# Two bias rows of the induced phase: one-row products into PSUM in place of GpSimd additions

## The chip, the core and the metric

The kernel runs on one core of a Trainium2 chip. Each engine has its own instruction stream: TensorE (PE, with weight loads shown apart as PEld), VectorE (DVE), ScalarE (ACT), GpSimd (POOL) and SyncE (SP, which only issues DMAs here). They wait for each other with semaphores, and each works strictly in its own order. TensorE writes its products to PSUM, eight banks of 128 partitions by 512 f32 numbers; VectorE and ScalarE empty the banks, and GpSimd works on SBUF alone. The metric is the time of one execution on the device in microseconds (us).

## The reference

A small model on 8 sequences (items) of 512 tokens: a two-layer banded-attention tower (D = 192), then an induced-set attention block with 128 inducing points (D = 128, 8 heads), then a mixture of 32 experts. The change lies in the second half of the attention block, `_mab(x, h, h, p2)`, for each item:

```python
def _mab(q, k, v, p):
    x = q + _mha(_ln(q, g1, b1), _ln(k, g1, b1), _ln(v, g1, b1), in_w, in_b, out_w, out_b)
    h = _ln(x, g2, b2)
    ff = gelu(h @ l1w.T + l1b) @ l2w.T + l2b
    return x + ff
```

`_mha` ends with `o @ out_w.T + out_b`. The two bias rows of the change are `out_b` and `l2_b` of this block, each of 128 numbers, added to all 512 tokens of an item. The block's result is added to the logits h of the tower, normalised, and goes to the gate of the experts.

## The kernel before

The kernel has three stages: embed and tower, the induced phase (function `induce`), and the experts. The induced phase works through the 8 items m in a software pipeline written out by hand. Time is cut into steps g; an item is PERIOD = 16 steps behind the one before it, and step g does for each item m the piece numbered p = g - 16 m. Every engine walks through the same steps, with the pieces of the older items first. A constant names the step of each piece (Y2 = 83, DOWN2 = 103, ...); an engine's order is the order of these numbers, and nothing else. So in the round in which item m is at Y2, item m-1 is at UP2 (99) and item m-3 scatters its rows (118 to 133).

An item's [512, 128] arrays are held as [128 partitions, NT = 4 tiles, E = 128], so one pass over an item is an instruction of 128x512. TensorE fills three PSUM banks in turn (`dense`, the tiles seam_dbank): `claim` waits until the bank's last content was copied, `filled` and `take` hand it over, `copied` and `wait_copied` give it back.

The pieces around the change, for item m:

- X2 (step 70): VectorE writes x2, the normalised input of the block (L1710), and signals x2_ready.
- X2_BIAS (79): GpSimd adds `out_b` to x2 in place (L1502) and signals x2b_ready.
- O2_T and Y2 (82, 83): TensorE turns the attention output, ScalarE copies it (o2T), TensorE multiplies it with wout (L1120, four products of 128 columns). VectorE adds x2 and writes y2 (L1907), its statistics (L1699, L1702) follow, GpSimd computes the inverse roots (L1446, L1448), and VectorE normalises to yn (L1710).
- Y2_SUM (85): GpSimd waits until item m-1's down2 bank was copied, computes y2b = y2 + h (L1509) and then adds `l2_b` (L1511).
- UP2 (99, 100): TensorE's up products (L1125), two and two, ScalarE's Gelu (L1639).
- DOWN2 (103): TensorE's sixteen down products (L1300); VectorE adds y2b and writes h2 (L1920), with statistics; GpSimd computes two inverse roots (L1454, L1455, L1458); VectorE normalises to zn and x5 (L1710).
- GATE to SLOT (114 to 117): gate products (L1316, L1317), top-2 selection on VectorE (L1756 to L1760, L1943, L1950, and L1946, for whose result ScalarE waits in L1651), slots (L1805, L1808).
- SCATTER (118 to 133): sixteen indirect DMAs issued by GpSimd (L1491).

In the same round as Y2_SUM of item m, item m+3 is at DOWN1 (38): its short root (L1446, L1448, one column) is GpSimd's next work behind y2b, and VectorE's short norm (R1_NORM, written to seam_v) and TensorE's transpose of it (L1114) wait for it.

The rows `erows` hold the bias rows spread over 128 partitions; `onerow` is one partition of 128 ones.

Of the kernel before, what the change touches and what calls it, by code (L numbers as in the profile page):

```python
# [11 lines left out]
ALU, ACT, AX = mybir.AluOpType, mybir.ActivationFunctionType, mybir.AxisListType  # L12

P = 128
B, S = 8, 512
NT = S // P
# [6 lines left out]
E = 128  # L23
IH = E // DH
IF = 512 // P
# [952 lines left out]
def induce(nc, a, outer, shared, seam, xs):  # L978
# [5 lines left out]
    with ExitStack() as ctx:  # L984
        ph = Phase(nc, "induce", ctx, outer)
# [4 lines left out]
        O1_OUT, O1_ROWS, O1_T, Y1, Y1_NORM, Y1_T = 22, 24, 26, 28, 31, 34  # L990
        UP1, DOWN1, R1_NORM, UK, K2, K2_STORE, Q_STACK, K2_STACK = 36, 38, 39, 42, 43, 50, 49, 55
        S2, M2, T2, V2 = (57, 59, 61, 63), 64, (69, 71, 73, 75), (72, 76)
        O2_OUT, O2_ROWS, O2_T, X2, X2_BIAS, Y2 = (73, 77), (75, 79), 82, 70, 79, 83
        Y2_MOM, Y2_NORM, Y2_SUM, Y2_T = 84, 93, 85, 95
        UP2, DOWN2, Z_NORM, X5_NORM, Z_ROWS, Z_T = (99, 100), 103, 106, 106, 108, 110
        GATE, GATE_1, GATE_2, Z_COPY, GATE_EXP, RANK, COEF, SLOT, STORE = 114, 115, 115, 119, 116, 117, 117, 117, 124
# [5 lines left out]
        NH, NV2 = 7, 3  # L1002
# [6 lines left out]
        erows = seam.wvo0[:, :].rearrange("p (b w e) -> p b w e", b=2, w=3)  # L1009
# [14 lines left out]
        onesr = shared.onerow[:, :].bitcast(F32)  # L1024

        def some(n, name, shape, dt=F32):
# [15 lines left out]
        h = list(seam.h)  # L1042

        scores, turned, dense, obank = seam.scores, seam.turned, seam.dense, seam.obank
# [3 lines left out]
        fore_set, consts_set, scaled = (ph.sem(n) for n in ("fore_set", "consts_set", "scaled"))  # L1048
        ones_in = [ph.sem(f"ones_in{j}") for j in range(2)]
        moments, roots, normed = ph.sem("moments"), ph.sem("roots"), ph.sem("normed")  # L1050
        x2_ready, x2b_ready, y1b_ready, x5_ready = (
            ph.sem(n) for n in ("x2_ready", "x2b_ready", "y1b_ready", "x5_ready"))
        split_hi, q1_hi, k2_hi = ph.sem("split_hi"), ph.sem("q1_hi"), ph.sem("k2_hi")
        q1_out, q1_in, kq_out, k2_out = (ph.sem(n) for n in ("q1_out", "q1_in", "kq_out", "k2_out"))
        k1_in, q2_in, k2_in = ([ph.sem(f"{n}{j}") for j in range(2)] for n in ("k1_in", "q2_in", "k2_in"))
# [10 lines left out]
        BV, BOUT, BL2 = range(3)  # L1066
# [42 lines left out]
        def on_tensor(pe, obank_left=None):  # L1109
# [7 lines left out]
            def by_rows(key, lhs, rhs, n=NT):  # L1117
                bank = dense.claim(pe, key)
                for t in range(n):
                    mm = pe.matmul(bank[:, t * E:t * E + E], lhs[:, t * P:t * P + P], rhs, start=True, stop=True)  # L1120
                dense.filled(mm, key)

            def by_features(key, w, rhs):
                bank = dense.claim(pe, key)
# [72 lines left out]
            def pieces(m, p):  # L1197
                if p == M1:
                    for head in (IH - 2, IH - 1):
                        scores.wait_copied(pe, ("s1", m, head))  # L1200
                    bank = dense.claim(pe, ("m1", m))
                    dense.filled(pe.transpose(bank[0:IH, 0:P], peak1[:, :], ident[:, :]), ("m1", m))
                if p == M2:
                    for head in (IH - 2, IH - 1):
                        scores.wait_copied(pe, ("s2", m, head))
                    bank = dense.claim(pe, ("m2", m))
                    dense.filled(pe.transpose(bank[0:IH * NT, 0:P], peak2[:, :], ident[:, :]), ("m2", m))
                if p == A_X:
                    pe.wait_ge(normed, norm_order[FINAL, m])
                    for k in range(KT):  # L1210
                        bank = dense.claim(pe, ("fT", m, k))
                        for t in range(NT):
                            mm = pe.transpose(bank[0:DP, t * P:t * P + P], xs[m][:, t, k * DP:k * DP + DP], ident[:, :])
                        dense.filled(mm, ("fT", m, k))
                if p == A_H:
                    for k in range(KT):
                        dense.wait_copied(pe, ("fT", m, k))
                    bank = dense.claim(pe, ("logits", m))
                    for t in range(NT):
                        for k in range(KT):  # L1220
                            mm = pe.matmul(bank[:, t * E:t * E + E], xT[:, k, t * P:t * P + P], wc[:, k, :],
                                           start=(k == 0), stop=(k == KT - 1))
# [12 lines left out]
                if p == O1_ROWS:  # L1235
                    outs.wait_copied(pe, ("o1", m))
                    bank = dense.claim(pe, ("o1R", m))
# [13 lines left out]
                if p == UP1:  # L1251
                    pe.wait_ge(ffn_in, FFN)
                    dense.wait_copied(pe, ("t1T", m))
                    bank = dense.claim(pe, ("up1", m))
# [27 lines left out]
                    turn(("o2T", m), o2)  # L1282
                if p == Y2:
                    dense.wait_copied(pe, ("o2T", m))
                    by_rows(("y2", m), o2T, wout[:, 1, :])
                if p == Y2_T:
                    pe.wait_ge(normed, norm_order[ATT2, m])
                    turn(("t2T", m), yn)
# [4 lines left out]
                if p == DOWN2:  # L1293
                    for c in range(IF):
                        dense.wait_copied(pe, ("up2", m, c))
                    bank = dense.claim(pe, ("down2", m))
                    for t in range(NT):
                        out = bank[:, t * E:t * E + E]
                        for c in range(IF):
                            mm = pe.matmul(out, hid2[:, c, t * P:t * P + P], l2[:, 1, c, :],  # L1300
                                           start=(c == 0), stop=(c == IF - 1))
                    dense.filled(mm, ("down2", m))
                if p == Z_T:
                    pe.wait_ge(normed, norm_order[FF2, m])
# [128 lines left out]
        def on_gpsimd(pool, chain=0, v_left=None):  # L1433
# [26 lines left out]
            def step(g):  # L1460
# [33 lines left out]
                for m, p in items(g):  # L1494
                    if p == Y1 + 1:
                        dense.wait_copied(pool, ("y1", m))
                        if m:
                            dense.wait_copied(pool, ("down1", m - 1))
                        pool.tensor_tensor(y1b[:, :], y1[:, 0, :], erows[:, 0, BL2, :], ALU.add).then_inc(y1b_ready, 1)
                    if p == X2_BIAS:  # L1500
                        pool.wait_ge(x2_ready, m + 1)
                        pool.tensor_tensor(x2[:, :, :], x2[:, :, :],  # L1502
                                           erows[:, 1, BOUT:BOUT + 1, :].broadcast_to([P, NT, E]), ALU.add)\
                            .then_inc(x2b_ready, 1)
                    if p == Y2_SUM:
                        dense.wait_copied(pool, ("y2", m))
                        if m:
                            dense.wait_copied(pool, ("down2", m - 1))
                        ch.mark(pool.tensor_tensor(y2b[:, :, :], y2[:, :, :], h[m % NH][:, :, :], ALU.add))  # L1509
                        ch.after()  # L1510
                        pool.tensor_tensor(y2b[:, :, :], y2b[:, :, :],  # L1511
                                           erows[:, 1, BL2:BL2 + 1, :].broadcast_to([P, NT, E]), ALU.add)\
                            .then_inc(y2b_ready, 1)
                    if p == Z_ROWS:
                        zm = z[m % 2]
                        if m == 0:
                            pool.wait_ge(late_in, LATE)
                        if m >= 2:
                            pool.wait_ge(scattered[m % 2], 16 * NT * SLOTS * (m // 2))
                        pool.wait_ge(normed, norm_order[FF2, m])  # L1520
                        first = zm[:, :, 0, 0:E]
                        ch.mark(pool.tensor_tensor(first, zn[:, :, :], grows[:, 0:1, :].broadcast_to([P, NT, E]),
                                                   ALU.mult))
                        ch.after()
                        pool.tensor_tensor(first, first, grows[:, 1:2, :].broadcast_to([P, NT, E]), ALU.add)\
                            .then_inc(z_ready, 1)
                        pool.tensor_scalar(zm[:, :, :, E:E + 1].bitcast(I32), ids[:, :, :, None], m * S * SLOTS, None,
                                           ALU.add).then_inc(z_named, 1)
                    if p == GATE:
                        pool.wait_ge(x5_ready, m + 1)  # L1530
                        if m:
                            pool.wait_ge(base_out, 16 * m)
                        pool.tensor_tensor(base[:, :, :], h2[:, :, :], x5[:, :, :], ALU.add).then_inc(base_ready, 1)
# [153 lines left out]
        def on_vector(dve, chain=0, x_final=None, xT_left=None, kq_left=None):  # L1687
# [125 lines left out]
            def pieces(m, p):  # L1813
# [88 lines left out]
                if p == Y2:  # L1902
                    bank = dense.take(dve, ("y2", m))
                    if m:
                        dve.wait_ge(y2b_ready, m)
                    dve.wait_ge(x2b_ready, m + 1)
                    dense.copied(dve.tensor_tensor(wide(y2), bank[:, :], wide(x2), ALU.add), ("y2", m))  # L1907
                if p == Y2_MOM:
                    dense.wait_copied(dve, ("y2", m))
# [598 lines left out]
```

## Time and profile before

| | |
|---|---|
| median of 3 runs | 2302.05 us (2300.82 to 2307.59) |
| profiled execution, its own time | 2290.77 us |
| its span, from the first to the last instruction | 2289.0 us |
| PE, PEld busy | 1994.3 us (87%), 1440.8 us (63%) |
| DVE, ACT, POOL busy | 1331.5 us (58%), 1171.7 us (51%), 779.3 us (34%) |
| mean granted TensorE clock | 0.909 |

Busy times are averages over the whole span. The three stages have different limits, so they are read by stretches. The granted clock is the share of full speed: 1.00 is 2.4 GHz and 0.50 is 1.2 GHz, and a mean between them is a mixture in time. In a timeline the columns are start, duration, engine, line, operation and tiles, with the count of merged instructions, and in brackets the engine's idle time before and what ended it. An f32 product leaves two records, so four products of one weight tile are eight records. "issue" is time in which the engine waited for nothing that the profile shows.

### The profile page before, as it was taken

The numbers are of one execution on the slowest core, as the hardware profiler recorded it, in microseconds if no ns is written. First come the engines' busy times: TensorE is split into PE (matmuls) and PEld (weight loads), VectorE is DVE, ScalarE is ACT, GpSimd is POOL, SyncE is SP. The second block draws the span as 40 slices with busy tenths as digits, with TensorE's granted clock in tenths as the row PEclk, the third lists the DMA queues.
The fourth block names the chain that finished last, engine by engine and source line by source line (L and its number), as shares of the span: only waits on it lengthen the run. The fifth ranks groups of instructions, "written<-read, shape, count | busy, mean of one in ns | idle before, by whom it ended". The sixth has DMA issues, their size and how long they took to land. (4 is left out here: it accounts for less than half of the span.)

```text
span 2289.0 us, 44262 instructions
## 1 busy us (share of the span) xinstructions
PE 1994.3 (87%) x14601; PEld 1440.8 (63%) x14601; DVE 1331.5 (58%) x4494; ACT 1171.7 (51%) x2507; POOL 779.3 (34%) x973
## 2 busy tenths in 40 slices
PE   5699999999999999999998878888876459999986
PEld 4366666666666666666666546656554349999973
DVE  2365565556556655565566645777766625555547
ACT  2376666566666665665666324555644224444434
POOL 0012221222122212221223221234787745555556
PEclk8799999999999999999999885798877579999995
DMA  3642441244134513440350124342321277777654
GB/s 101 123 72 28 70 71 38 34 70 70 33 40 70 94 30 43 70 69 27 47 88 11 34 70 83 86 92 49 80 57 37 76 247 234 231 228 228 200 157 129
DMA packets 113846, 207.06 MB, mean 90 GB/s; under 512 B 23060, under 2 KB 47510, under 8 KB 112968
## 3 DMA queue, kind: packets, MB, share of 16 engines
q1 hardware_dynamic: 100632, 182.97, 36.0%
q0 software_dynamic: 10176, 17.09, 2.3%
q10 hardware_dynamic: 2816, 4.16, 0.6%
q8 instruction: 124, 2.03, 0.4%
q14 instruction: 98, 0.80, 0.1%
HBM read 147.53 MB, written 64.66 MB: 93 GB/s over the span
## 5 line engine op out<-in xcount | busy, mean ns | idle before, releaser
L733 ACT ACTIVATE tower_prob<-tower_prob,tower_negmax 128x386 f32<-128x386 f32 (+1 forms) x768 | 390.5, 556 | 312.0 <-DVE tower_negmax L943 311.4
L943 DVE CUSTOM_DVE_ANT_0 tower_prob<-seam_sbank,tower_band 128x386 f32<-128x386 f32 (+1 forms) x768 | 346.1, 488 | 138.7 <-PE seam_sbank L496 133.3
L534 PEld LDWEIGHTS seam_tbank<-sh_ident,tower_prob 128*128 128x128 f32 x1920 | 226.3, 142 | 131.0 <-issue 81.0
L534 PE MATMUL seam_tbank<-sh_ident,tower_prob 128*128 128x128 f32 x1920 | 283.0, 278 | 23.5 <-DVE seam_probT L968 21.3
L789 ACT ACTIVATE seam_probT<-seam_tbank 128x384 f32<-128x384 f32 (+1 forms) x576 | 227.5, 430 | 123.6 <-PE seam_tbank L534 121.3
L2186 POOL DMA_INDIRECT scratch_yt<-experts_y,experts_rows x190 | 186.7, 983 | 183.6 <-DVE experts_y L2329 151.1
L473 PE MATMUL seam_dbank<-tower_oxT,tower_w 96*128 96x512 f32 x384 | 190.9, 621 | 14.7 <-ACT tower_oxT L778 14.7
L496 PE MATMUL seam_sbank<-seam_k_st,seam_q_st 49*128 49x386 f32 (+1 forms) x768 | 160.1, 411 | 30.0 <-POOL seam_k_st L684 16.3
L2244 PE MATMUL experts_ybank<-experts_w,experts_hid 128*128 128x128 f32 x1520 | 185.1, 275 | 0.0
L2232 PE MATMUL experts_hbank<-experts_zT,experts_w 128*128 128x256 f32 x760 | 181.5, 382 | 1.1 <-ACT experts_zT L2268 1.1
L2277 ACT ACTIVATE experts_hid<-experts_hbank,experts_w 128x256 f32<-128x256 f32 x190 | 79.8, 471 | 193.9 <-PE experts_hbank L2232 193.9
L2244 PEld LDWEIGHTS experts_ybank<-experts_w,experts_hid 128*128 128x128 f32 x1520 | 177.2, 192 | 0.1
L700 POOL TENSOR_TENSOR tower_glob<-tower_vglob,tower_prob 128x102 f32<-128x102 f32 x128 | 46.8, 365 | 338.6 <-ACT tower_prob L733 224.2
L2232 PEld LDWEIGHTS experts_hbank<-experts_zT,experts_w 128*128 128x128 f32 x760 | 138.3, 192 | 16.7 <-issue 1.7
L393 PE MATMUL seam_dbank<-tower_w,tower_hid 128*128 128x192 f32 x768 | 141.0, 334 | 4.5 <-DVE tower_hid L917 4.5
L513 PE MATMUL seam_obank<-seam_probT,seam_v 128*17 128x128 f32 x3840 | 142.8, 276 | 1.6 <-DVE seam_probT L968 1.6
L2314 DVE TENSOR_SCALAR experts_hid<-experts_hbank,experts_w 128x256 f32<-128x256 f32 x190 | 83.2, 479 | 103.6 <-PE experts_hbank L2232 103.6
L1491 POOL DMA_INDIRECT scratch_zs<-induce_z,induce_slot x128 | 127.5, 996 | 36.6 <-issue 34.3
L496 PEld LDWEIGHTS seam_sbank<-seam_k_st,seam_q_st 49*128 49x128 f32 x768 | 73.9, 184 | 98.5 <-issue 85.3
L412 PE MATMUL seam_dbank<-seam_xT,seam_wqk 96*96 96x512 f32 x256 | 129.4, 632 | 5.6 <-ACT seam_xT L748 5.6
L393 PEld LDWEIGHTS seam_dbank<-tower_w,tower_hid 128*128 128x128 f32 x768 | 123.1, 190 | 17.8 <-issue 9.6
L1547 ACT ACTIVATE seam_probT<-seam_tbank 128x512 f32<-128x512 f32 x128 | 69.6, 597 | 100.6 <-PE seam_tbank L1182 64.2
(329 smaller groups left out, 3441.0 us busy)
## 6 DMA issues: line engine op xcount, KB each, us to landing
experts_w<-ew SPq DMA_DIRECT2D x95, 578.0 KB, 4.0
scratch_qk<-seam_qk SPq DMA_DIRECT2D x64, 384.0 KB, 4.7
seam_q_st<-scratch_qk SPq DMA_DIRECT2D x96, 192.0 KB, 8.3
seam_k_st<-scratch_qk SPq DMA_DIRECT2D x96, 192.0 KB, 11.6
experts_rows<-scratch_zs SPq DMA_DIRECT2D x95, 132.0 KB
scratch_kq<-seam_qk SPq DMA_DIRECT2D x8, 1024.0 KB, 4.3
experts_res<-scratch_yt SPq DMA_DIRECT2D x8, 1024.0 KB, 7.9
seam_q_st<-scratch_kq SPq DMA_DIRECT2D x48, 128.0 KB, 4.3
```

Source lines behind the costliest of these rows:

```text
L393: mm = pe.matmul(bank[:, j * D:(j + 1) * D], lhs[:, k, t * P:t * P + P], rhs[:, k, :], start=(k == 0), stop=(k == kts - 1))
L412: mm = pe.matmul(bank[0:DP, :], wqk[layer][:, w, k, c * DP:c * DP + DP], xT[:, k, :], start=(k == 0), stop=(k == KT - 1))
L473: mm = pe.matmul(bank[:, :], w1[:, k, c * P:c * P + P], oxT[:, k, :], start=(k == 0), stop=(k == KT - 1))
L496: mm = pe.matmul(bank[:, 0:width(i)], stack(q_st[j], h0 + e)[:, i * P:i * P + P], stack(k_st[j], h0 + e)[:, first_key(i):first_key(i) + wi ...
L513: mm = pe.matmul(obank[32 * e:32 * e + W17, c:c + P], v[nq % 2][:, t, h0 + e, :], probT[(2 * gq + e) % PT][:, jb * P:jb * P + P], start=(j ...
L534: mm = pe.transpose(bank[:, jb * P:jb * P + P], prob[:, hg % PR, at + jb * P:at + jb * P + P], ident[:, :])
L733: act.activation(prob[:, hg % PR, 0:width(i)], prob[:, hg % PR, 0:width(i)], ACT.Exp, bias=negmax[:, hg % PR:hg % PR + 1], scale=-1.0).the ...
L789: turned.copied(act.activation(probT[(2 * (g - 1) + e) % PT][:, 0:at], bank[:, 0:at], ACT.Copy), ("t", g - 1, e))
L943: scores.copied(dve.tensor_tensor_reduce(prob[:, hg % PR, 0:width(i)], bank[:, 0:width(i)], band[:, BAND_AT[i]:BAND_AT[i] + width(i)], sca ...
L2186: pool.indirect_dma_start(out=a["yt"], out_offset=bass.IndirectOffsetOnAxis(ap=rows[q % ZB][:, h, E:E + 1].bitcast(U32), axis=0), in_=y[q ...
L2232: mm = pe.matmul(bank[:, j * TB:j * TB + TB], w[q % WW][:, W1 + c * P:W1 + c * P + P], zT[q % 2][:, :], start=True, stop=True)
L2244: mm = pe.matmul(bank[:, h * E:h * E + E], hid[q1 % 2][:, c, h * P:h * P + P], w[q1 % WW][:, W2 + c * E:W2 + c * E + E], start=(c == 0), s ...
```

## The change

GpSimd's two additions of a bias row (L1502 and L1511, once an item) go. In their place TensorE starts the bank of y2, and that of down2, with one product: a column of ones (one partition, 128 weights) times the bias row (one partition, 128 numbers, read four times over, 512 columns), which writes the whole bank. The products that follow accumulate on it. VectorE's y2 addition waits for x2_ready in place of x2b_ready. No step number is moved.

```diff
@@ step numbers
-        O2_OUT, O2_ROWS, O2_T, X2, X2_BIAS, Y2 = (73, 77), (75, 79), 82, 70, 79, 83
+        O2_OUT, O2_ROWS, O2_T, X2, Y2 = (73, 77), (75, 79), 82, 70, 83
@@ TensorE
+            def on_rows(bank, row):
+
+                pe.matmul(bank[:, :].rearrange("p (t e) -> p t e", e=E), onesr,
+                          erows[0:1, 1, row:row + 1, :].broadcast_to([1, NT, E]), start=True, stop=False,
+                          skip_group_check=True)
...
                 if p == Y2:
                     dense.wait_copied(pe, ("o2T", m))
-                    by_rows(("y2", m), o2T, wout[:, 1, :])
+                    bank = dense.claim(pe, ("y2", m))
+                    on_rows(bank, BOUT)
+                    for t in range(NT):
+                        mm = pe.matmul(bank[:, t * E:t * E + E], o2T[:, t * P:t * P + P], wout[:, 1, :],
+                                       start=False, stop=True, skip_group_check=True)
+                    dense.filled(mm, ("y2", m))
...
                     bank = dense.claim(pe, ("down2", m))
+                    on_rows(bank, BL2)
                     for t in range(NT):
                         out = bank[:, t * E:t * E + E]
                         for c in range(IF):
                             mm = pe.matmul(out, hid2[:, c, t * P:t * P + P], l2[:, 1, c, :],
-                                           start=(c == 0), stop=(c == IF - 1))
+                                           start=False, stop=(c == IF - 1), skip_group_check=True)
@@ GpSimd
-                    if p == X2_BIAS:
-                        pool.wait_ge(x2_ready, m + 1)
-                        pool.tensor_tensor(x2[:, :, :], x2[:, :, :],
-                                           erows[:, 1, BOUT:BOUT + 1, :].broadcast_to([P, NT, E]), ALU.add)\
-                            .then_inc(x2b_ready, 1)
                     if p == Y2_SUM:
                         dense.wait_copied(pool, ("y2", m))
                         if m:
                             dense.wait_copied(pool, ("down2", m - 1))
-                        ch.mark(pool.tensor_tensor(y2b[:, :, :], y2[:, :, :], h[m % NH][:, :, :], ALU.add))
-                        ch.after()
-                        pool.tensor_tensor(y2b[:, :, :], y2b[:, :, :],
-                                           erows[:, 1, BL2:BL2 + 1, :].broadcast_to([P, NT, E]), ALU.add)\
+                        pool.tensor_tensor(y2b[:, :, :], y2[:, :, :], h[m % NH][:, :, :], ALU.add)\
                             .then_inc(y2b_ready, 1)
@@ VectorE
                     if m:
                         dve.wait_ge(y2b_ready, m)
-                    dve.wait_ge(x2b_ready, m + 1)
+                    dve.wait_ge(x2_ready, m + 1)
                     dense.copied(dve.tensor_tensor(wide(y2), bank[:, :], wide(x2), ALU.add), ("y2", m))
```

## Rows read from the trace of the kernel before

**Rows 1.** Windows: busy us (and count) of each engine, granted clock, DMA share, GB/s.

```profile
core 0: us, PE busy (x) PEld busy (x) DVE busy (x) ACT busy (x) POOL busy (x), PEclk, DMA share, GB/s
1450.00:1735.00 285.00, 235.78 (x1712) 164.48 (x1715) 212.96 (x663) 158.28 (x271) 148.71 (x172) 0.82 0.31 69
1735.00:1850.00 115.00, 46.18 (x215) 34.70 (x207) 61.09 (x207) 27.29 (x35) 89.26 (x92) 0.63 0.27 84
1850.00:2289.00 439.00, 403.08 (x2566) 353.55 (x2566) 227.98 (x683) 174.52 (x452) 226.72 (x231) 0.91 0.67 207
```

**Rows 2.** Timeline of POOL at the end of the induced phase.

```profile
1845.91 0.95 POOL L1491 DMA_INDIRECT scratch_zs<-induce_z,induce_slot  x1 [0.30 <-issue]
1850.06 0.10 POOL L2180 MEMSET experts_half<- 128x8 f32 x1 [3.19 <-POOLq L984]
```

**Rows 3.** Waits of DVE from 1370 to 1850 us: us in total, times, longest.

```profile
DVE induce_zn L1710 <- POOL seam_padrow_f L1458: 22.2, 7, 5.3
...
DVE seam_v L1710 <- POOL seam_padrow_f L1448: 14.2, 8, 2.4
DVE induce_h L1920 <- PE seam_dbank L1300: 11.0, 6, 3.7
```

**Rows 4.** Timeline of all engines, item 2's h2 and item 3's y2b.

```profile
1620.40 0.69 DVE L1920 TENSOR_TENSOR induce_h<-seam_dbank,induce_y2b 128x512 f32<-128x512 f32 x1 [1.49 <-PE seam_dbank L1300]
...
1621.24 1.26 POOL L1509 TENSOR_TENSOR induce_y2b<-induce_y,seam_qk_f 128x512 f32<-128x512 f32 x1 [4.13 <-DVE induce_h L1920]
...
1622.59 1.26 POOL L1511 TENSOR_TENSOR induce_y2b<-induce_y2b,seam_wvo 128x512 f32<-128x512 f32 x1
...
1623.82 0.23 POOL L1446 TENSOR_SCALAR seam_padrow_f<-seam_padrow_f 128x1 f32<-128x1 f32 x1
...
1624.85 0.35 DVE L1710 TENSOR_SCALAR seam_v<-seam_v,seam_padrow_f 128x128 f32<-128x128 f32 x1 [2.43 <-POOL seam_padrow_f L1448]
...
1625.25 0.48 PE L1114 MATMUL seam_dbank<-sh_ident,seam_v 128*128 128x128 f32 x1 [2.66 <-DVE seam_v L1710]
```

**Rows 5.** Timelines of DVE, POOL and ACT where L1502 or L1511 runs.

```profile
1492.51 3.15 DVE L1710 TENSOR_SCALAR induce_x<-seam_qk_f,seam_padrow_f 128x128 f32<-128x128 f32 x4
...
1509.25 2.13 DVE L1710 TENSOR_SCALAR induce_yn<-induce_y,seam_padrow_f 128x128 f32<-128x128 f32 x4
...
1678.00 0.32 DVE L1758 TENSOR_TENSOR induce_ga<-induce_ga,induce_rank 128x160 f32<-128x160 f32 x1
...
1680.15 1.86 DVE L1758 TENSOR_TENSOR induce_gb<-induce_gb,induce_rank 128x160 f32<-128x160 f32 x1
...
1680.54 1.28 POOL L1502 TENSOR_TENSOR induce_x<-induce_x,seam_wvo 128x512 f32<-128x512 f32 x1
...
1722.58 0.22 ACT L1651 ACTIVATE induce_gs<-induce_gs 128x20 f32<-128x20 f32 x1 [1.48 <-DVE induce_gs L1946]
```

**Rows 6.** Timeline of PE: two f32 products of 512 columns, at either clock.

```profile
1520.05 1.99 PE L1125 MATMUL seam_dbank<-induce_t,induce_l 128*128 128x512 f32 x4
1521.87 1.05 PE L1120 MATMUL seam_dbank<-induce_wout,induce_o2T 128*128 128x128 f32 x8
...
1604.05 3.63 PE L1125 MATMUL seam_dbank<-induce_t,induce_l 128*128 128x512 f32 x4
```

**Rows 7.** Line L424 in the tower: duration ns min/median/max, first and last start.

```profile
L424 PE MATMUL seam_dbank<-seam_padrow,sh_onerow x16: 489/494/501, 50.5 to 1163.1; 1*128 1x512 f32 x16
```

**Rows 8.** Timelines around y2: DVE in item 2, PE and ACT in item 4.

```profile
1569.79 0.69 DVE L1907 TENSOR_TENSOR induce_y<-seam_dbank,induce_x 128x512 f32<-128x512 f32 x1 [2.11 <-PE seam_dbank L1120]
...
1646.01 1.88 PE L1125 MATMUL seam_dbank<-induce_t,induce_l 128*128 128x512 f32 x4
...
1648.86 1.27 ACT L1639 ACTIVATE induce_hid<-seam_dbank,induce_l1b 128x512 f32<-128x512 f32 x2
```

**Rows 9.** Windows behind two gaps of TensorE, columns as in Rows 1.

```profile
1499.00:1502.00 3.00, 2.41 (x20) 1.81 (x20) 2.24 (x7) 0.94 (x3) 0.00 (x0) 1.00 0.60 233
...
1587.00:1593.00 6.00, 5.00 (x27) 3.00 (x26) 4.28 (x12) 1.86 (x5) 5.01 (x7) 0.50 0.25 83
```

**Rows 10.** Timeline of PE behind item 0's y2b.

```profile
1498.67 0.27 PE L1202 MATMUL seam_dbank<-sh_ident,seam_rows 128*8 128x128 f32 x1 [1.57 <-DVE seam_qk L1716]
```

More of the change, by code:

```diff
@@ L1050, in induce @@
         moments, roots, normed = ph.sem("moments"), ph.sem("roots"), ph.sem("normed")
-        x2_ready, x2b_ready, y1b_ready, x5_ready = (
-            ph.sem(n) for n in ("x2_ready", "x2b_ready", "y1b_ready", "x5_ready"))
+        x2_ready, y1b_ready, x5_ready = (ph.sem(n) for n in ("x2_ready", "y1b_ready", "x5_ready"))
         split_hi, q1_hi, k2_hi = ph.sem("split_hi"), ph.sem("q1_hi"), ph.sem("k2_hi")
```

## The prediction

> **What bounds the kernel now.** I read the busy shares by stage first [rows 1]. The first 1370 us (embedding and tower) and the last 439 us (the experts) hold none of the changed instructions, so the change is worth what it does between 1450 and 1850 us. There no engine is full. From 1450 to 1735 us TensorE is busy 235.8 of 285 us at a granted clock of 0.82 (its two levels are 1.2 and 2.4 GHz, so about a third of that stretch is at the lower one), VectorE 213.0 and GpSimd only 148.7. From 1735 to 1850 us GpSimd leads with 89.3 of 115 us. The stage ends with GpSimd's last scatter, and the experts' first GpSimd instruction comes 3.2 us behind it [rows 2]. So the path goes from engine to engine, and the waits have to be read.
>
> The waits of VectorE in this stage [rows 3] show GpSimd as a link: 22.2 us in 7 waits before zn and 14.2 us in 8 before the short norms, both for the inverse roots that GpSimd computes; and 11.0 us in 6 waits on the second down product. One item in order of time [rows 4] shows how they hang together. VectorE waits 1.49 us for L1300 and makes h2 (L1920). Only then may GpSimd start the next item's y2b (L1509; it had waited 4.13 us). It adds the bias (L1511), and only then comes to the root (L1446) that VectorE has been waiting for: 2.43 us. TensorE, behind VectorE, has stood idle for 2.66 us. The removed L1511 stands in this chain with nothing beside it. L1502, the other removed addition, lies elsewhere, before the y2 addition.
>
> **What the change removes.** L1511, 8 times. In [rows 4] the root starts at 1623.82; without L1511 it would start at the end of L1509, 1622.50: 1.3 us. Items 1 to 7 have this order, items 1 to 4 with a short root next and items 5 to 7 with the root of zn. VectorE's wait of 2.43 us is longer than 1.3 us, as are the seven before zn on average (22.2/7 = 3.2 us), so the gain is passed on whole: 7 x 1.3 = 9.1 us. If the released root then waits for something else, the gain is nothing; that is the other bound.
>
> L1502, 8 times about 1.28 us. GpSimd rarely makes anybody wait with it, but VectorE suffers under it [rows 5]: its L1758 of 128x160, otherwise 0.32 us, takes 1.86 us when L1502 starts inside it. Four more items (3, 4, 6, 7) show one such VectorE instruction of 1.8 to 2.1 us there. In most of them the y2 addition behind it has to wait for TensorE in the new kernel anyhow, so I count nothing. Three places count. In item 6 the stall reaches ScalarE, which waits 1.48 us for VectorE; I take 1.2 us. In item 1 four norms take 2.13 us in place of 1.1 and TensorE waits for them 0.85 us: 0.8. In item 0 four norms take 3.15 us beside both y2b additions, half of the 2.0 us too much being L1511's: 1.0. Together 3.0 us; bounds 0 and 5 x 1.5 + 1.0 + 1.0 = 9.5.
>
> **What it adds.** Sixteen products of one row by 128x512, f32. No row of this kernel has one. The nearest are the 128-row products L1125 [rows 6]: two of them are four records (an f32 product leaves two), and the next product starts 1.82 us after the first, so 0.91 us each at 2.4 GHz; at 1.2 GHz the same four take 3.63 us in place of 1.99, some 1.7 us each. A one-row product exists in the tower, L424, in the one-pass type: its one record lasts 494 ns [rows 7], while one of the 128-row L1125 lasts about 0.6, so the missing rows save little. I take 0.91 and bound it by 0.49 below and 1.7 above. The Trainium skill, "TensorE: Matmul & The Clock Gate", section Back-to-back issue gap, gives about 216 ns for 512 columns at the upper clock; taken for each of the two records that would be an estimate of 0.43 us for a product, and the sum below would be some 5 us better. The trace has 0.455 us per record, about double, and it decides.
>
> The product ahead of down2 stands between the up products' copies, which TensorE waits for first, and L1300. Behind it are VectorE's h2, y2b and the roots. Paid eight times: 8 x 0.91 = 7.3 us. In two of the eight h2 does not wait for TensorE (6 waits in [rows 3]), so some of the product is covered there: minus 0.9.
>
> The product ahead of y2 stands behind the wait for o2T. Queued behind it on TensorE are the second pair of up products and the next scores. In items 0, 1 and 2 VectorE waits for TensorE at y2 already (2.11 us in item 2 [rows 8]) and TensorE runs on without a gap, so it is paid: 0.91 + 0.91 + 1.7 (item 2 has the lower clock there) = 3.5 us. In items 3 to 7 there is cover: in item 4 the second up pair ends at 1647.89, but ScalarE, loading activation tables, copies it only from 1648.86, 0.97 us later [rows 8], more than 0.91. Without this cover it would be another 5 x 0.91 = 4.6 us.
>
> The accumulating start=False changes no count of products. The y2 addition now waits for x2_ready, VectorE's own norm 13 steps earlier: nothing. The y2b semaphore comes earlier.
>
> Sum: -9.1 - 3.0 + 7.3 - 0.9 + 3.5 = -2.2 us. The profiled execution has 2290.8 us with a span of 2289.0, so 2288.6; the runs' median stands 11.3 us above it, so the same sum is made against the median: 2302.05 - 2.2 = 2299.8 us. I call anything within 0.3% (6.9 us) no change, about what a measurement of this kernel can tell.
>
> **Rivals.**
>
> *A, the clock stays up: faster.* In the 2.66 us gap of [rows 4] and the three like it (items 1, 2, 4) the granted clock falls to 1.2 GHz and stays there for 6 to 9 us; from 1587 to 1593 us TensorE is busy 5.0 of 6 us at 0.50 [rows 9]. In item 0's round the same gap was 1.57 us [rows 10], and the clock stayed at 1.00 [rows 9]. The change makes 2.66 into about 1.35. If all four falls go, some 4 x 5.0 us of work take half the time; of the 10 us I count 7 to 8, as part ends in other waits: 2299.8 - 7.5 = 2292. Against it: the clock also falls in gapless stretches of transposes and narrow gate products, so a fall may only come later. The same page of the Trainium skill, section The HAM clock gate, says that idleness lowers the clock and sustained activity restores it, by which shorter gaps and more products both help; the fall in a 2.66 us gap agrees, and no row shows whether a one-row product counts as activity.
>
> *B, TensorE pays more: slower.* Place: the product ahead of L1300. It pays for itself only while it costs less than the 1.3 us that L1511 gives back. If TensorE is at 1.2 GHz there, it costs 1.7 us: 8 x 0.8 = 6.4 us more, and if the cover at y2 is gone too, 4.6 more. 2299.8 + 6.4 + 4.6 = 2310.8. It decides from about 1.5 us a paid product on. For it: the clock is low at the start of the last down products. Against it: in items 0 to 3 L1300 runs at 2.4 GHz.
>
> *C, the roots are not freed:* the gap behind L1509 is filled by a wait on VectorE's statistics and the 9.1 us shrink to half: 2304. Against it: the short root's statistics are long done in [rows 4]. It stays within 0.3%.
>
> **How the numbers follow.** My sum, with C and halves of A and B, stays within 0.3%: 0.47. A whole, or a bias product that is cheaper than its 128-row kin: 0.33. B: 0.20. Range: low end below A, 2288; high end at B, 2312. The likeliest case alone: 2295 to 2306.
>
> **What the profile after would show.** L1502 and L1511 gone, 32 new one-row records of 0.5 to 0.6 us. VectorE's waits before zn down from 22.2 to about 13 us and before the short norms from 14.2 to about 9 or 10; TensorE's gaps of 2.66 us and the like near 1.4. VectorE's wait for L1300 up from 11.0 by some 5 us. The 1.8 to 2.1 us VectorE instructions before y2 back at 0.3. The granted clock from 1450 to 1735 us: 0.82 in my sum, 0.88 or more under A, under 0.80 under B. I am wrong if the shortened wait reappears at the next link, if the new products bunch where nothing covers them, or if the clock moves by its own timing.

## The result, and the profile after

The changed kernel takes 2308.8 us (median of 15 executions) against 2298.9 us for the one before (15 executions): 1.0055 times as long, 95% interval 1.0035 to 1.0074 (the medians alone give 1.0043, which lies inside). That is slower by more than the 0.3% that I called no change. The time lies inside the range, 9.0 us above the value I gave, on the side of rival B, which had the smallest chance (0.20).

The profiled execution of the changed kernel took 2321.6 us, 13 us above its median, and the one of before stood 8 us below its own. So the two profiles exaggerate: they differ by 31 us, the medians by 10. They show where the time goes, not how much; a second profile of the changed kernel, which differs from this one, stands under experiment 2.

Windows of the changed kernel, columns as in [rows 1]:

```profile
1450.00:1735.00 285.00, 254.82 (x1623) 168.78 (x1622) 185.53 (x593) 144.41 (x251) 112.60 (x139) 0.75 0.30 64
1735.00:1850.00 115.00, 80.29 (x339) 55.78 (x335) 71.53 (x252) 42.32 (x55) 84.97 (x90) 0.65 0.13 43
```

Against [rows 1], TensorE is busier (254.8 us for 235.8) and has got through fewer instructions (1623 for 1712), although it has the bias products besides. The granted clock goes with both: 0.75 in place of 0.82. VectorE and GpSimd were busy for less of the same time (185.5 us for 213.0, and 112.6 for 148.7), GpSimd in part because its additions are gone.

Waits of VectorE in the changed kernel, 1370 to 1850 us, as in [rows 3]:

```profile
DVE induce_h L1923 <- PE seam_dbank L1311: 28.9, 8, 6.2
...
DVE induce_y L1910 <- PE seam_dbank L1293: 22.1, 7, 6.9
DVE induce_zn L1713 <- POOL seam_padrow_f L1469: 15.9, 6, 3.7
...
DVE seam_v L1713 <- POOL seam_padrow_f L1459: 7.7, 7, 1.1
```

The bottom two rows are the intended effect. The wait before the short norms falls from 14.2 to 7.7 us, the longest from 2.4 to 1.1 us, by the 1.3 us of L1511. The wait before zn falls from 22.2 to 15.9 us. The top two are the price: the wait for the down product goes from 11.0 to 28.9 us, and the y2 addition, for which the waits of before had 5.5 us in three items, now waits 22.1 us in seven.

Two f32 records make a product. Line L1124 of the changed kernel between 1450 and 1850 us: busy us, mean ns of a record:

```profile
L1124 PE MATMUL seam_dbank<-seam_wvo,sh_onerow 1*128 1x512 f32 x32 | 24.2, 845 | 3.1 <-ACT induce_hid L1642 3.1
```

and two such pairs in its timeline, one at each clock:

```profile
1485.52 1.12 PE L1124 MATMUL seam_dbank<-seam_wvo,sh_onerow 1*128 1x512 f32 x2
1486.57 1.16 PE L1293 MATMUL seam_dbank<-induce_wout,induce_o2T 128*128 128x128 f32 x8
1487.66 0.69 PE L1162 MATMUL seam_sbank<-seam_q_st 48*128 48x512 f32 x2
...
1626.08 2.07 PE L1124 MATMUL seam_dbank<-seam_wvo,sh_onerow 1*128 1x512 f32 x2
```

The projection starts 1.05 us after the bias product: that is its price at 2.4 GHz (I had 0.91). All 32 records make 24.2 us of TensorE's time, 1.5 us a product. That leaves the clock to look at. Windows of the changed kernel around that first product and in its longest stretches at 1.2 GHz:

```profile
1480.00:1487.00 7.00, 6.76 (x76) 4.79 (x76) 5.24 (x17) 3.69 (x9) 2.04 (x3) 1.00 0.02 5
1488.00:1491.00 3.00, 3.00 (x26) 2.38 (x28) 3.00 (x10) 0.61 (x3) 0.00 (x0) 0.50 1.08 148
1505.00:1528.00 23.00, 23.00 (x136) 16.37 (x128) 13.08 (x37) 9.16 (x16) 3.55 (x7) 0.50 0.39 56
1601.00:1630.00 29.00, 26.71 (x143) 18.51 (x144) 17.00 (x42) 13.49 (x22) 17.73 (x20) 0.50 0.36 90
1690.00:1716.00 26.00, 26.00 (x95) 16.25 (x93) 18.18 (x58) 11.20 (x16) 19.09 (x20) 0.50 0.35 76
```

In this profile the clock falls behind the first product although TensorE had been busy 6.76 of 7 us, and it stays low for 23 to 29 us at a time with TensorE busy nearly all through. In the profile of before, from 1485 to 1798 us, the low stretches last 3 to 10 us, but for two of 17 and 20. A low clock beside a busy TensorE is not new, though. The kernel before has it ahead of these items, where no bias product runs:

```profile
1437.00:1460.00 23.00, 21.68 (x152) 17.31 (x154) 16.49 (x47) 9.95 (x19) 4.58 (x8) 0.50 0.46 92
```

So two theories stand. **Added work**: TensorE pays the products' own time, and the clock is an accident. **Clock**: the one-row products make the granted clock fall more often than their own time explains, and everything behind them pays.

### The profile page after: what moved, and what is told of

It is laid out like the page before. It is cut to its first block and busy times, and to the rows that moved or that the text cites. A ratio compares the mean times of both kernels' runs of the same rounds, so it can differ in the third digit from the quotient of the medians.

```text
span 2319.8 us, 44310 instructions
## 1 busy us (share of the span) xinstructions
PE 2047.1 (88%) x14633; PEld 1465.1 (63%) x14633; DVE 1323.5 (57%) x4494; ACT 1173.1 (51%) x2507; POOL 758.2 (33%) x957
## 5 line engine op out<-in xcount | busy, mean ns | idle before, releaser
L1502 POOL DMA_INDIRECT scratch_zs<-induce_z,induce_slot x128 | 127.1, 993 | 37.4 <-issue 35.2
```

## The experiments

Each ratio is against the kernel before, timed on the same chip beside the experiment. From group to group the kernel before moved by more than the effect: 2328.5, 2326.3, 2300.4, 2298.1 and 2299.7 us in the five groups below. A price in us is the ratio's distance from 1, or from another ratio, times about 2300 us, unless it is said to be from medians.

**1. The halves, the gain alone, the price alone.** e1 has the product and the freed GpSimd for y2 only, e2 for down2 only. e3 leaves both biases out of the computation. e4 keeps GpSimd's additions and throws the products away:

```diff
 # shortened. e3: no product, no addition; e4, on the kernel before:
-                    on_rows(bank, BOUT)
-                    on_rows(bank, BL2)
+ pe.matmul(bank, onesr, row, start=True, stop=True)   # ahead of both projections
+ ... projections with start=True: they overwrite it
```

> The change's first half alone: the output projection's bias goes into PSUM as a one-row product and GpSimd's addition to x2 is gone; GpSimd keeps the addition of the second bias to y2b. The change as a whole measured 1.0055 times before. Three theories. (1) Added work: each product costs its own time on TensorE at the clock of the moment (a pair of records took 1.12 us at 2.4 GHz and 2.07 us at 1.2 GHz in the profile after), nothing else. Of y2's eight products nearly all are paid, since the later profile shows VectorE waiting for TensorE at y2 in seven of eight items: +9 to +13 us, less 3 us for the removed addition's stalls: ratio 1.003 to 1.004. (2) Clock: a one-row product is a stretch in which TensorE counts as idle, and the granted clock falls more often after it: more than the products' own time is lost, ratio 1.004 or more, and the granted clock of 1450 to 1735 us falls below 0.79. (3) My prediction's terms: +3.5 - 3.0 = +0.5 us, ratio 1.000.

> The second half alone: the bias of the last projection goes into PSUM as a one-row product, GpSimd's second addition on y2b is gone; the addition to x2 stays with GpSimd and y2 has no product. (1) Added work: eight products of 0.9 to 2 us by the clock, +8 to +13 us, against 1.3 us x 7 that the root comes earlier: ratio 0.999 to 1.002. (2) Clock: as for the first half, ratio above 1.003 with a granted clock below 0.79 in 1450 to 1735 us. (3) My prediction's terms: -9.1 + 7.3 - 0.9 = -2.7 us, ratio 0.999.

> Leaves work out: neither bias of the induced phase is added by anyone (no one-row products, no additions on GpSimd). What is left is what freeing GpSimd is worth. By my prediction's terms -9.1 - 3.0 = -12 us, ratio 0.995. If GpSimd's additions lay beside other work, 1.000. With the added-work theory this run and the next one should add up to the change as a whole: (ratio here - 1) + (ratio of the next - 1) = 0.0055. If the sum is far less than the change, the two halves meet: an earlier root brings TensorE's work together where the products then stand in the way.

> The kernel before, with both one-row products put ahead of the projections and overwritten by them (the projections start their banks anew), and GpSimd's additions all kept: the price of the products alone. (1) Added work: 16 products of 0.9 to 2.07 us, most of them paid: +14 to +22 us, ratio 1.006 to 1.010, granted clock of 1450 to 1735 us about as before (0.80 to 0.84). (2) Clock: ratio above 1.010, granted clock below 0.79. (3) My prediction's terms: +7.3 + 3.5 = +10.8 us at most, ratio 1.0047 or less.

Measured: e1 1.0007 (0.9990 to 1.0024), e2 1.0000 (0.9981 to 1.0018), e3 0.9933 (0.9908 to 0.9958), e4 1.0086 (1.0061 to 1.0111). Freeing GpSimd is worth 15.6 us (11.7 by medians) where I had 12.1. The products cost 20 us where I had 9.9. Each half fits my terms (+0.5 and -2.7 us) within its interval; the whole does not, and is not the sum of its halves. Both theories have misses here. Added work fits e2 and e4, but for e1 it asked for 1.003 to 1.004, above the interval. The clock theory's values were missed in e1 (1.004 or more), e2 (above 1.003) and e4 (above 1.010, just inside the interval); the clocks that it asked for from 1450 to 1735 us, below 0.79, came in the profiles of e2 and e4 (0.78 each) and not in that of e1 (0.82).

**2. Rows and places.** Beside the changed kernel again (e5), e6 makes the same products from 128 rows: weights of 1/128 and the bias from every partition, the same 512 columns.

```diff
-                pe.matmul(bank[:, :].rearrange("p (t e) -> p t e", e=E), onesr,
-                          erows[0:1, 1, row:row + 1, :].broadcast_to([1, NT, E]), start=True, stop=False,
+                pe.matmul(bank[:, :].rearrange("p (t e) -> p t e", e=E), share[:, :],
+                          erows[:, 1, row:row + 1, :].broadcast_to([P, NT, E]), start=True, stop=False,
```

e7 issues the one-row products ahead of the waits:

```diff
-                    dense.wait_copied(pe, ("o2T", m))
                     bank = dense.claim(pe, ("y2", m))
                     on_rows(bank, BOUT)
+                    dense.wait_copied(pe, ("o2T", m))
```

(and the same for down2's four waits). e8 has no product at all: on the kernel before, GpSimd adds the second bias to h ahead of time.

```diff
+                        pool.tensor_tensor(h[m % NH], h[m % NH], BL2 row, ALU.add)   # shortened; behind L1502
-                        pool.tensor_tensor(y2b, y2b, BL2 row, ALU.add)               # L1511
```

> The changed kernel itself, on the chip of the three runs after it, so that they stand beside it. The first call gave 1.0007 for y2's half, 1.000 for down2's half, 0.9933 with both biases left out and 1.0086 with the products alone: products and freed GpSimd add up to 1.0019, the halves to 1.0007, and the whole had measured 1.0055 on another chip. If the pieces add up, this run gives 1.001 to 1.003; if the halves hurt each other, 1.0045 to 1.0065 again.

> The change, with the same 16 products made of all 128 rows (weights of 1/128, the bias from every partition) in place of one row: the same columns, the same two records a product, 128 times as many cells at work. (1) Added work: a product costs what it did, but for a weight load of 128 rows: within 0.15% of the changed kernel. (2) Clock: if one-row products count as idleness to whatever grants the clock, the granted clock of 1450 to 1735 us rises from below 0.79 to 0.82 or more and the time falls by 10 us or more, ratio 0.4% below the changed kernel's.

> The change, with each product issued ahead of the waits that it stood behind: y2's before the wait for o2T's copy, down2's before the waits for the four Gelus. The work of every engine is the same, only its place moves. (1) Added work on the path between the last copy and the first product of the projection: taking it off that path gives back nearly all, since TensorE waits there in any case: ratio 0.993 to 0.997. If TensorE had no wait there (it arrives late itself), the product costs the same at either place and the ratio stays that of the changed kernel. (2) Clock by one-row products: ratio above 1.002, as the products are still there.

> No product on TensorE at all: the second bias is added by GpSimd to h, ahead of time, right behind the addition to x2, so that only one addition is left between y2 and y2b. It asks for the part of my sum that frees the root of the last norm alone: -9.1 us there, and one more early GpSimd addition of 1.3 us beside VectorE (+0 to +3 us of stalls): ratio 0.996 to 0.9985. If what the run without biases gained came from the other addition, ratio 1.000.

Measured: e5 1.0041 (1.0016 to 1.0066), e6 0.9941 (0.9918 to 0.9963), e7 0.9991 (0.9969 to 1.0013), e8 0.9954 (0.9932 to 0.9975). The 128-row products make the same change 1.0% faster, where added work alone allowed 0.15%. e8 measures one term of my sum alone: -10.6 us, where I had -9.1 before any stall of the moved addition. e7 says that the place matters too: some 12 us of the one-row products' price go when they are issued in the wait (7 us by medians). That was neither theory's value: added work asked for 0.993 to 0.997, or for no change, and the clock theory for more than 1.002.

The products' busy time is not what changed. Line L1124 of e5, then of e6, between 1450 and 1850 us:

```profile
L1124 PE MATMUL seam_dbank<-seam_wvo,sh_onerow 1*128 1x512 f32 x32 | 21.6, 760 | 3.1 <-ACT induce_hid L1642 3.1
```

```profile
L1124 PE MATMUL seam_dbank<-seam_wvo,induce_share 128*128 128x512 f32 x32 | 21.5, 760 | 3.5 <-ACT induce_hid L1644 2.1 <-issue 1.4
```

But the next product starts a little sooner behind 128 rows, here at 2.4 GHz, e5 and then e6:

```profile
1525.63 1.12 PE L1124 MATMUL seam_dbank<-seam_wvo,sh_onerow 1*128 1x512 f32 x2
1526.68 1.16 PE L1293 MATMUL seam_dbank<-induce_wout,induce_o2T 128*128 128x128 f32 x8
```

```profile
1523.36 1.02 PE L1124 MATMUL seam_dbank<-seam_wvo,induce_share 128*128 128x512 f32 x2
1524.22 1.05 PE L1294 MATMUL seam_dbank<-induce_wout,induce_o2T 128*128 128x128 f32 x8
```

That is 1.05 us behind one row and 0.86 behind 128 (0.96 at other places); at 1.2 GHz it is 2.00 against 1.71 to 1.87. With 16 products at 0.09 to 0.29 us each I estimate 1 to 5 us from this, of the 19 us between e5 and e6.

The clock of these two profiles does not show what the theory asked for. e5 is the changed kernel again, in an execution 7 us below its median; e6's is 7 us below its own too. The stretch of the items in e5, then the 43 us from its first bias product on:

```profile
1485.00:1800.00 315.00, 261.03 (x1648) 175.86 (x1646) 210.03 (x687) 155.39 (x256) 156.55 (x181) 0.79 0.25 57
1492.00:1535.00 43.00, 38.58 (x341) 25.34 (x339) 33.39 (x100) 29.00 (x55) 11.12 (x17) 1.00 0.51 95
```

The stretch of the items in e6:

```profile
1485.00:1800.00 315.00, 262.83 (x1677) 178.53 (x1676) 218.48 (x726) 163.04 (x266) 172.52 (x197) 0.79 0.26 60
```

Both stand at 0.79, and from 1450 to 1735 us at 0.81 and 0.82, where the theory wanted e5 below 0.79. Behind e5's first product, at 1492.39 us, the clock does not fall: it holds 1.00 to 1535 us. So the fall behind the first product in the profile after is one execution's, not the rule. From 1485 us up to the last scatter (1874 and 1853 us) the clock is 0.74 in e5 and 0.76 in e6, which makes 202 and 177 us at 1.2 GHz.

**3. How far the rows carry.** e9 is e4 with 128 rows, e10 the change with 32 rows (`share[0:32, :]`, weights of 1/32), e11 has y2's bias by a 128-row product and the second as in e8, e12 is e6 with the products ahead of the waits as in e7.

> The kernel before with 16 products of 128 rows added and overwritten, GpSimd's additions kept: the run that gave 1.0086 (+20 us) with one-row products, with rows changed alone. (1) Added work: the columns and records are the same, so the price is the same: ratio 1.006 to 1.011. (2) Clock: in the change as a whole 128 rows in place of one gave 0.9941 against 1.0041; if that is the clock, which counts a one-row product as little or no work, the price here falls to less than half, ratio 1.000 to 1.004, with the granted clock of 1485 to 1800 us higher than with one-row products at the same place.

> The change with products of 32 rows. (2) Clock, by share of the rows at work: between one row (1.0041) and 128 rows (0.9941), ratio 1.000 to 1.003. If a threshold in rows decides and 32 are enough, 0.992 to 0.996; if 32 are as bad as one, 1.002 to 1.006. (1) Added work: no dependence on rows at all, and then the 128-row run's 0.9941 must have been something else.

> A candidate for the best version: y2's bias by a 128-row product on TensorE, the second bias added to h by GpSimd ahead of time in the place of the addition to x2, so TensorE has eight products instead of sixteen and the root of the last norm has one addition ahead of it. The 128-row version gave 0.9941, the h version 0.9954, both biases left out 0.9933. Expected 0.992 to 0.996; if 128-row products gain by themselves (they keep the clock up), this is worse than the 16-product version, 0.995 or more.

> The 128-row version with each product issued ahead of the waits of its projection. With one-row products the move took 1.0041 to 0.9991. (1) Added work: the products of the 128-row version are still on the path, so the move gives 5 us or so again: ratio 0.990 to 0.993. (2) Clock: the waits before the projections are filled with work that counts, ratio also 0.990 to 0.993 and a granted clock above 0.80 in 1485 to 1800 us. If the 128-row version already pays nothing for its products (it stood 0.0008 above the version without biases), the move changes nothing: 0.993 to 0.996.

Measured: e9 1.0064 (1.0042 to 1.0087), e10 1.0019 (0.9999 to 1.0040), e11 0.9953 (0.9935 to 0.9971), e12 0.9962 (0.9948 to 0.9977). 32 rows are slower than 128 clear of the intervals; that they are faster than one is not (1.0019 against 1.0055, 1.0041 and 1.0032), and the next product starts 1.05 us behind them, as behind one row. The place, worth 12 us to one-row products, is worth nothing to 128-row ones. But e9 missed: with GpSimd's additions in place, the rows are worth 0.2% as measured (1.0086 against 1.0064 in two groups of runs, the intervals overlap), not the half of the price that the clock theory asked for. (The granted clock from 1485 to 1800 us did go up, 0.75 to 0.78.)

**4. Was it the rows?** e6 also has one more tile, one more memset and one more wait. h13 has all three and takes one row of that tile. h14 repeats the 128-row version, h15 the kernel before. h16 has one row for y2 and 128 for down2.

```diff
-                          ... share[:, :],   erows[:, 1, row:row + 1, :].broadcast_to([P, NT, E]),
+                          ... share[0:1, :], erows[0:1, 1, row:row + 1, :].broadcast_to([1, NT, E]),
```

> Everything that the 128-row version has beside the rows (a tile of 64 KB more in SBUF ahead of the others, its memset, the wait at y2), with products of one row of that tile. If the rows decide: 1.003 to 1.007, as the changed kernel. If the layout or the memset made the 128-row version fast: 0.992 to 0.997.

> The 128-row version again: 0.992 to 0.997 if its 0.9941 stands. A value of 1.000 or more would make its first measurement chance.

> The kernel before against itself: 1.000, within 0.003 either way. Where it lies outside, differences of 0.3 per cent in this series say nothing.

> Both products, y2's with one row, down2's with 128. Behind down2 TensorE has other items' work, ahead of it the longest wait (four Gelus). If the rows of both matter alike: half way, 0.998 to 1.001. If down2's product decides: 0.993 to 0.997. If y2's does: 1.002 to 1.006.

Measured: h13 1.0032 (1.0007 to 1.0057), h14 0.9966 (0.9950 to 0.9981), h15 0.9986 (0.9969 to 1.0003), h16 0.9984 (0.9972 to 0.9997). It was the rows: h13's interval and h14's do not touch. The kernel before against itself shows how much 0.14% is worth. The profile of h13 repeats the waits of the first profile of the changed kernel to 0.1 us; both are of long executions, h13's the longest of its ten. In e5 the same two waits are 23.4 and 13.4 us, in e6 17.9 and 8.5. Waits of VectorE, h13 and then h14:

```profile
DVE induce_h L1925 <- PE seam_dbank L1312: 28.9, 8, 6.2
...
DVE induce_y L1912 <- PE seam_dbank L1294: 22.1, 7, 6.9
```

```profile
DVE induce_h L1925 <- PE seam_dbank L1312: 18.4, 7, 4.3
...
DVE induce_y L1912 <- PE seam_dbank L1294: 14.0, 7, 3.4
```

**5. Which product, and what is left of the price.** h17 is the mirror of h16. h18 is e3 again.

> 128 rows for y2, one row for down2. One row for y2 and 128 for down2 gave 0.9984, half way between 0.9955 (mean of the two 128-row runs) and 1.0043 (mean of the three one-row runs). If the two products weigh alike, 0.998 to 1.002 here too; if down2's one-row product carries most of it, 1.001 to 1.004; if y2's does, 0.994 to 0.997.

> Leaves both biases of the induced phase out, no products and no additions, as before. If the 128-row products cost their own time (16 x 1.1 us, half of it covered), this is 0.3 to 0.5 per cent below their version: 0.990 to 0.993. If they are nearly free, 0.993 to 0.996.

Measured: h17 1.0004 (0.9984 to 1.0023), h18 0.9937 (0.9914 to 0.9961). Waits of VectorE in h18:

```profile
DVE induce_zn L1707 <- POOL seam_padrow_f L1463: 19.1, 7, 4.9
...
DVE induce_h L1917 <- PE seam_dbank L1305: 15.0, 6, 3.4
DVE seam_v L1707 <- POOL seam_padrow_f L1453: 8.8, 8, 1.1
...
DVE induce_y L1904 <- PE seam_dbank L1119: 5.5, 4, 2.5
```

Now the price has a floor to be measured from, 0.9935 (mean of e3 and h18):

| version | ratio | above the floor | mean granted clock, less that of before in the same group |
|---|---|---|---|
| no bias (e3, h18) | 0.9933, 0.9937 | 0 | +0.0031, +0.0018 |
| 128 rows (e6, h14) | 0.9941, 0.9966 | 0.0019 = 4 us | +0.0049, +0.0019 |
| 1 row y2, 128 rows down2 (h16) | 0.9984 | 0.0049 = 11 us | +0.0021 |
| 128 rows y2, 1 row down2 (h17) | 1.0004 | 0.0069 = 16 us | -0.0007 |
| 1 row (after, e5, h13) | 1.0055, 1.0041, 1.0032 | 0.0108 = 25 us | -, -0.0021, -0.0025 |

The clock is the mean over a whole execution, averaged over the 7 to 33 executions of each. Taking the eight products of one bias from 128 rows to one costs 7 to 14 us, for down2 (12 and 14 us) clear of the intervals; for y2 (7 and 9 us) they overlap. The clock goes down with it in three of the four steps; from h14 to h16 it does not (+0.0019 and +0.0021, in the same group).

The window from 1485 to 1800 us holds the eight items. In h18, h15 (before), h14 and h13:

```profile
1485.00:1800.00 315.00, 252.66 (x1723) 180.55 (x1723) 227.62 (x758) 166.61 (x273) 181.72 (x209) 0.81 0.28 64
```

```profile
1485.00:1800.00 315.00, 248.36 (x1674) 175.23 (x1673) 228.99 (x729) 163.97 (x267) 192.06 (x213) 0.80 0.26 60
```

```profile
1485.00:1800.00 315.00, 265.16 (x1695) 180.48 (x1695) 220.91 (x728) 164.56 (x268) 171.25 (x196) 0.79 0.26 60
```

```profile
1485.00:1800.00 315.00, 277.56 (x1567) 184.24 (x1567) 201.75 (x670) 154.49 (x253) 152.19 (x176) 0.72 0.25 57
```

From h14 to h13 the clock goes from 0.79 to 0.72, and TensorE gets through 1567 products where it had 1695. Of these 128, though, some 80 are the work of 1485 to 1491 us in h14, where the items start 6 us later (first bias product at 1492.5 us, for 1486.5 in h13); some 50 are left. And e5, with the same one-row products, stood at 0.79. The means over all executions are the better witness, and they point the same way by less. A mean lower by 0.0044 (0.9049 in h14, 0.9005 in h13), at a low level of half speed, is 0.0044 x 2300 / 0.5 = 20 us more at 1.2 GHz, in which TensorE gets 10 us less done. From e6 to e5 it is 0.0069 (0.9012, 0.8943): 32 us and 16 us. The times differ by 17.5 and 19.3 us (medians). These are estimates of the most that the clock can explain, as if every such microsecond delayed the end. So the clock is large enough for most of the difference; the earlier start behind 128 rows has 1 to 5 us of it by my estimate; and items that arrive late may stand in each other's way. The three were not separated. Nor does a long low stretch need a one-row product; h18 has no bias product at all:

```profile
1665.00:1685.00 20.00, 19.92 (x89) 14.55 (x88) 13.89 (x40) 7.86 (x13) 16.26 (x17) 0.50 0.31 66
```

## Why the prediction was wrong

**What the change removes.** Right, and sized a little low: 12.1 us predicted, 14.5 and 15.6 measured (h18, e3; 14.1 and 11.7 by medians); the part of L1511 alone 9.1 predicted, 10.6 measured (e8). Its signs came too: the wait before the short norms at 7.7 us (I gave 9 to 10), the one before zn at 15.9 us (about 13), TensorE's gaps of 2.7 to 3 us down to 1.20, 1.31 and 1.70 us.

**What it adds.** Here the prediction failed, at the step that follows "the missing rows save little": the price of the 128-row kin, 0.91 us, was made the price of the one-row product, +9.9 us in the sum. The sentence itself holds, the missing rows save nothing; they cost. The next product starts 1.05 us behind one row and 0.86 to 0.96 us behind 128, and the whole kernel is 17 to 19 us slower with one row. With the kin itself in its place, 16 products cost 4 us, less than my 9.9, so more of them was covered than I had counted; with one row they cost 25 us. VectorE's wait for L1300, for which I gave 5 us more, took 17.9 more in the first profile. The bounds, 0.49 and 1.7 us a product, were bounds of the product's own time and did not hold the cost. I had written that no row shows whether a one-row product counts as activity, and then gave the question to rival A's benefit only, for which more products were to help.

**The cover at y2.** I had it in items 3 to 7, under ScalarE's table loads. The y2 addition waits in seven items in the first profile of the changed kernel, and with 128 rows in seven (h14, 14.0 us in all) or four (e6, 8.5 us), against 5.5 us without biases (h18). So this cover was an error too, but a small one in time: with 128 rows the whole price is 4 us.

**Rival A, the clock stays up.** Wrong in its step from gap to fall. The gaps became short as it asked, and even without any product (h18, e3) the clock from 1485 to 1800 us is 0.81 and 0.79 against 0.80 before. The falls stay or move. And the changed kernel has the lower clock; it stands at 0.50 for 23 us with TensorE busy 23.00 of them. The Trainium skill, "TensorE: Matmul & The Clock Gate", section The HAM clock gate, ties the clock to how busy TensorE has been. By busy time alone that stretch would not stand at 0.50, so the trace disagrees, and it decides. I had also written that I am wrong if the clock moves by its own timing. In part it does: the same kernel fell behind its first product in one profile and held 1.00 there in another (e5).

**Rival B, TensorE pays more.** It gave 2310.8 us and a granted clock under 0.80; measured were 2308.8 and 0.75, but 0.81 in e5's profile. Both conditions are seen in part in the first profile: eight of the sixteen products meet the low clock, and y2's cover is gone in seven items. But its mechanism, the products' own time at 1.2 GHz, applies nearly as well to 128 rows (1.71 to 1.87 us against 2.00), which cost 4 us. So its number came close by luck: it named the place, not the cause. Rival C did not happen: the roots are freed.

**What stays open.** Why rows matter little while GpSimd's additions remain (e4 and e9, 0.2% with overlapping intervals), and with that why the halves cost 0 to 2 us and the whole 7 to 13. And the link itself: that the rows act through the clock is argued, from the mean clock measured lower in both pairs. Against it stand the equal 0.79 of e5's and e6's profiles and the step from h14 to h16. A lower clock can also be in part the effect of a kernel that waits more, and no run held the clock fixed. The later start behind 1 and 32 rows is a rival for part of the price that no run removed.

**The better versions.** With 128 rows the change does what it was meant to, as measured against the kernel before: 0.9941 and 0.9966. The one without TensorE (e8, 0.9954) and the mixed one (e11, 0.9953) are as good, and cannot be told apart from it here. All lie within 0.4% of the floor.

## What to carry to other kernels

The price of a product is more than the time that it occupies TensorE: in a kernel whose TensorE moves between 1.2 and 2.4 GHz, look also at the mean granted clock over many executions, since two profiles of one kernel can differ (0.72 and 0.79 here). Try a bias product from all 128 rows (weights of 1/128, the bias on every partition) beside the one-row form: here it had the same busy time and took 0.7 and 1.0% off the kernel's time. When such a change is priced, a run that leaves the work out altogether gives the floor, and one that adds the work alone gives the price; halves that look free say nothing of the whole.

## What the runs showed of the hardware

The granted clock stood at 0.50 for 23 and 26 us in which TensorE was busy all the time (changed kernel, 1505 to 1528 and 1690 to 1716 us), and for 20 us in which it was busy 19.92, with no bias product in the kernel (h18, 1665 to 1685 us). The number of rows of a product changes the kernel's time: 1 row 1.0043 (mean of three), 32 rows 1.0019, 128 rows 0.9954 times before (mean of two). Two f32 records of 512 columns let the next product start after 1.05 us with 1 or 32 rows, and after 0.86 to 0.96 us with 128, at 2.4 GHz. One kernel can have its low stretches in different places: in the 43 to 45 us from its first bias product on, the changed kernel's clock was 1.00 in e5's profile (1492 to 1535 us) and 0.70 in the first (1485 to 1530 us). And the same kernel took 2328.5 us in one group of runs and 2298.1 us in another, 1.3% apart, so only ratios within a group were compared.
